# A pairwise-interaction tower on one core: more halves folded, most of them by accumulating transfers, and the sums in another order

## The reference, cut to what matters

```
e = stack([tbl_f[ids[:, f]] for f in range(40)], axis=1)     # 512 x 40 x 64
i_idx, j_idx = triu_indices(40, k=1)                         # 780 pairs
viW = einsum('bpd,pde->bpe', e[:, i_idx, :], W)              # a 64x64 matrix for each pair
z   = einsum('bpe,bpe->bp', viW, e[:, j_idx, :])             # 512 x 780
h = relu(concat([z, dense_ctx]) @ W_top1 + b_top1)           # 796 -> 512
h = relu(h @ W_top2 + b_top2)                                # 512 -> 256
y = h @ W_top3                                               # 256 -> 1
```

## Time and profile before

| | |
|---|---|
| time, median of 3 runs | 334.14 us (334.05 to 335.86) |
| the profiled execution's own time | 336.78 us |
| its span, first to last instruction | 334.9 us |
| granted TensorE clock | 1.00 throughout |
| PE, DVE, ACT, POOL busy | 325.1, 262.9, 199.5, 227.9 us |
| DMA share, mean of 16 engines; moved | 28.77 MB, 86 GB/s |

### The profile page before, as it was taken

The page is one execution under the profiler, slowest core; times in us unless marked ns, Lnnn a source line. Parts: engine busy times, 40 slices in busy tenths (PEclk is TensorE's granted clock), DMA queues, the critical chain, the costliest instruction groups (busy, mean ns, idle before and its releaser), DMA issues.

```text
span 334.9 us, 5224 instructions
## 1 busy us (share of the span) xinstructions
PE 325.1 (97%) x1614; PEld 113.1 (34%) x1614; DVE 262.9 (79%) x245; ACT 199.5 (60%) x1140; POOL 227.9 (68%) x180
## 2 busy tenths in 40 slices
PE   7999999999999999979999999999999999999996
PEld 2244333333333333323333223232333333333342
DVE  2979997786898979848996997968988879888031
ACT  1378633313406794649998993568968495495131
POOL 5665654665667774768888889876996998667000
PEclk9999999999999999999999999999999999999999
DMA  7656331321574754544730320203204000000000
GB/s 190 258 192 217 86 85 20 113 85 25 143 172 88 176 138 89 131 94 135 275 111 18 110 75 6 78 5 116 70 1 113 16 1 0 2 1 0 2 0 0
DMA packets 12479, 28.77 MB, mean 86 GB/s; under 512 B 3730, under 2 KB 4500, under 8 KB 12324
## 3 DMA queue, kind: packets, MB, share of 16 engines
q1 hardware_dynamic: 7060, 20.04, 18.1%
q0 software_dynamic: 5248, 8.40, 12.9%
q10 hardware_dynamic: 144, 0.00, 0.0%
HBM read 24.24 MB, written 0.00 MB: 72 GB/s over the span
## 4 chain that ended last, share of the span: by engine, by line
PE 52%; POOL 18%; DMA 17%; issue 9%; ACT 3%; DVE 1%; POOLq 0%
PE u L665 24%; POOL gath L467 18%; DMA gath<-in_tbl,ids_sb 14%; PE zp L690 8%; PE u L653 6%; PE u L726 4%; PE xp L704 4%; ACT prod L545 2%; PE u L766 2%; DMA prod<-prod 2%; PE u L642 1%; PE xp L610 1%; DMA ids_sb<-in_ids 1%; DVE prod L833 0%; DVE prod L822 0%
## 5 line engine op out<-in xcount | busy, mean ns | idle before, releaser
L833 DVE TENSOR_TENSOR prod<-u,xq_part 128x1024 f32<-128x1024 f32 x148 | 172.6, 1217 | 29.8 <-PE u L665 20.6
L467 POOL DMA_INDIRECT gath<-in_tbl,ids_sb x128 | 126.0, 985 | 69.7 <-DMA gath<-in_tbl,ids_sb 36.5
L665 PE MATMUL u<-xt,w_ring 64*128 64x512 f32 x632 | 162.0, 618 | 0.8 <-DVE prod L833 0.3
L545 ACT ACTIVATE prod<-prod 128x64 f32<-128x64 f32 x512 | 122.7, 242 | 17.0 <-DVE prod L815 12.8
L484 POOL TENSOR_TENSOR prod<-prod 128x1024 f32<-128x1024 f32 x40 | 93.6, 2364 | 10.6 <-DVE prod L833 10.3
L545 ACT ACTIVATION_READ_ACCUMULATOR prod<-prod 128x1 f32 x512 | 96.0, 188 | 0.3 <-issue 0.2
L665 PEld LDWEIGHTS u<-xt,w_ring 64*128 64x128 f32 x632 | 53.3, 185 | 96.4 <-DVE prod L833 40.7
L690 PE MATMUL zp<-prod,sel_sb 128*32 128x512 f32 x480 | 58.5, 599 | 2.5 <-DMA prod<-prod 2.3
L529 ACT ACTIVATE xq_part<-xt 32x512 f32<-32x512 f32 x72 | 45.2, 627 | 1.7
L523 ACT ACTIVATE xt<-xp 128x512 f32<-128x512 f32 x20 | 11.8, 591 | 56.0 <-PE xp L610 44.7
L815 DVE TENSOR_TENSOR prod<-u,gath 128x1024 f32<-128x1024 f32 x32 | 38.9, 1217 | 5.3 <-PE u L653 5.3
(11 more groups left out here) (42 smaller groups left out, 109.0 us busy)
## 6 DMA issues: line engine op xcount, KB each, us to landing
w_ring<-in_w_cell SPq DMA_DIRECT2D x20, 512.0 KB
prod<-prod POOLq DMA_DIRECT2D x8, 512.0 KB
late<-in_ids_small SPq DMA_DIRECT2D x4, 512.0 KB, 5.5
gath<-in_tbl,ids_sb POOLq DMA_INDIRECT x128
wide_w<-in_w_wide SPq DMA_DIRECT2D x8, 256.0 KB
late<-in_w_top SPq DMA_DIRECT2D x1, 1792.0 KB
late<-in_small SPq DMA_DIRECT2D x3, 512.0 KB
wd_sb<-in_w_diag SPq DMA_DIRECT2D x1, 640.0 KB
```

Of the source, the lines that this page charges most:

```text
L467: pool.indirect_dma_start(gath[:, place, t, half, :], None, tables[f], bass.IndirectOffsetOnAxis(ap=ids_sb[:, t, f:f + 1], axis=0),).then_ ...
L545: total = act.activation(part, part, ACT.Copy, accum_out=zw_sb[:, t, 2 * HF * j + pair:2 * HF * j + pair + 1])
L665: mm = pe.matmul(u[:, n % UR, a, :], w_ring[rows, q % RW, at * P:(at + 1) * P], xt[rows, moving % XR, :], start=True, stop=True)
L833: dve.tensor_tensor(prod[:, n % PR, :, :], u[:, n % UR, :, :], x, ALU.mult).then_inc(prod_ready, 1)
```

## The change

Three things change, all by tables and by the order of a list. First, `FOLDED` and `DMA_BELOW`: all units of blocks 12 to 15 are folded, 54 units in all instead of 48. Those of blocks 8 to 15 are folded by transfer, 28 instead of 8; GpSimd's own adds go from 40 to 26. Second, `BATCHES` is sorted by the slot in which a batch can be summed. A plain batch or a quad no longer stands behind a folded one that gets ready later. `places` then puts the rows elsewhere in the banks, and the top weights' rows follow. Third, `FOLDS_AFTER` and `EARLY_AT` are new.

```diff
-FOLDED = {4: 2, 5: 2, 6: 3, 7: 4, 8: 6, 9: 7}
-DMA_BELOW = 6
-FOLDS_AFTER = [0] * 12 + [1, 1, 1, 1, 1, 1, 0, 2, 0, 2, 2, 2, 1, 3, 3, 4, 0, 7, 0, 0]
+FOLDED = {4: 2, 5: 2, 6: 4, 7: 6, 8: 6, 9: 7}
+DMA_BELOW = 8
+FOLDS_AFTER = [0] * 12 + [1, 1, 1, 1, 1, 1, 1, 1, 2, 2, 3, 1, 2, 2, 4, 4, 2, 4, 5, 0]
+LAG = 4
+FOLD_LAG = 12
+def natural_slot(batch):
+    what, m, units, folded = batch
+    last = QUAD_END[m] if what == "quad" else max(AT[("unit",) + u + (HI,)] for u in units)
+    return last + (FOLD_LAG if folded else LAG)
 def batches_in_order():
-    return out
+    return sorted(out, key=natural_slot)
-EARLY_AT = [131, 131, 135, 142, 148, 153, 164, 164, 169, 182, 187, 187]
+EARLY_AT = [129, 140, 140, 144, 147, 147, 166, 166, 166, 181, 184, 193]
```

More of the change, by code:

```diff
@@ L189 @@
 GROUPS = groups()
-LAG = 4
-FOLD_LAG = 12
 def sum_slots():
```

## The result

The changed kernel takes 339.55 us (median of 6, 339.03 to 340.6), the kernel before 335.8 us on the same chip: a ratio of 1.012 [1.0096, 1.0143]. It is slower, by 1.2%. The forecast was 337.0 us, a range of 329 to 343.5, and slower as the likeliest outcome. It was the time before as known then, 334.14 us, plus 2.9; on 335.8 the same 2.9 would have made it 338.7.

A forecast was written before the change was run, and what follows sets the result against it. VectorE was taken to set the pace, with the transfers due before slot 137's round deciding. A delay of +0.25 us there and +2.6 for early steps made +2.9 on 334.14: 337.0 us, range 329 to 343.5.

The forecast's parts named there:

- The mechanism: Up to slot 137: the 10.8 us gained by rounds and order are eaten by waits for transfers on the DMA engines.
- The price of a fold by transfer: DMA engines: one fold by transfer costs 2.75 us, between bounds of 2.6 and 2.9; 20 new ones cost 55 us.
- The first waits: Behind slots 88 and 94: folds beside the top layer's weights last until 168.3 us, and the lead of 6.1 is gone.
- Rounds and order: Slots 39 to 137: fewer rounds and sorted sums gain 6.1 us by slot 82, 10.8 by slot 137, if nothing else waits.
- the ledger: TensorE's lead over VectorE: extra work adds debt, each slot repays 0.27 us, and what exceeds 1.1 us is lost.
- The delay at slot 138: Round behind slot 137 can't start before 223.7 us, when its last transfer is seen; TensorE goes on 0.25 us later.
- rival 3: DMA engines pause between bursts, as a half's gathers must land before the next half's issue: 8.5 us more, 345; 15%.
- The early steps: Behind slot 137: 11 early steps instead of 9, closer together, lose 10.5 us where 7.9 were lost, so 2.6 more.
- rival 2: Transfers bind, but late steps cost nothing, their lost lead covered by earlier waits for ScalarE: 334.4 us; chance 15%.
- The sum: Whole kernel: +0.25 us at slot 138 and +2.6 for the early steps make +2.9, so 337.0 us.
- GpSimd at nothing: GpSimd: 14 adds fewer (33 us less) and 20 issues more (20 us more) costed at nothing; 13 gained if on the path.
- 1: Transfers are never waited for, so 8.2 us are gained: 326 us; 20% for this side as a whole.

## Why the prediction held, and where it didn't

*The mechanism, right.* The order's gain is eaten by waits for the new transfers beside the top layer's weights. The transfers with half their bytes (333.87 us) show that it is the bytes, and the sorted kernel without the 20 new ones (333.63 us, old tables) agrees.

*The price of a fold by transfer, right.* GpSimd's queue had 12.9% of the 16 engines in a span of 334.9 us before, and has 28.5% of 338.3 now. That is 43.2 and 96.4 us, and 53.2 more for 20 transfers: 2.66 us each, against 2.75. (The gathers are on the same queue and are taken to cost the same in both.)

*The first waits, right in place.* Behind slot 94 the folds were to land at 168.3 us, and TensorE started at 169.09. "The lead of 6.1 is gone there" holds and says too little: a lead of 4.6 became 7.1 us behind at slot 95.

*Rounds and order, about right.* Up to slot 82 a gain of 6.1 us was predicted, 4.6 measured; the ledger's 5.7 us of gaps were 6.8. For slots 83 to 137 the ledger has a gain of 4.7. From slot 95 to 107 the changed kernel took 15.06 us where it was 16.73, a gain of 1.7 (the ledger has 1.6 for slots 83 to 107), and from 107 to 138 39.50 where it was 41.86, a gain of 2.4 (3.1 in the ledger), with the waits of 0.90 and 0.26 in it. Half of these 4.0 us are the early steps that moved behind slot 137: with the old places 2.0 are regained (from 173.43 at slot 95 to 230.02 at slot 138, 56.6 us against 58.6). Sorting alone gained hardly anything there (2.2 us at slot 82, 2.6 at slot 138).

*The delay at slot 138, mis-sized: +0.25 predicted, +3.1 measured.* The step was "Even with no pause the last transfer is through at 223.3", a lower bound that I took for the value. The last transfer landed at 226.4 (the chain of the kernel after has it from 213.28 us on, for 13.10 us). The first new one was issued 1.2 us later than I had it (146.19, not 145.0), but the price of 2.66 in place of 2.75 takes 1.8 off. What is left is pauses. The DMA window of the kernel after (length, granted clock, DMA share, GB/s):

```profile
146.50:226.00 79.50, 0.94 0.96 219
```

Four hundredths of 79.5 us are 3.2 us. The longest pause lies in 180 to 185 us, with a share of 0.44: one transfer was issued at 175.12, and the next stood behind the four gathers of the half that followed, until 183.13, and waited for no product. That is the mechanism of rival 3, at less than half its size.

*The path to that delay, and a term left out.* I had TensorE reach slot 137 with its gain and wait there for the last transfer. It waited 0.26 us there. The gain was lost at slots 88 and 94, 11.7 us between slots 82 and 95, and 2.2 to 2.3 of these are the clock, which was not in my sum at all. I had worked out the landing at 168.3 and didn't carry it on. Shown is that the stall suffices by itself: 7.54 us of waiting and the clock at half behind it lead to the same place (228.54) in a kernel with 16 transfers, the last of them issued at 175.16 us. The two bounds, the stall carried on and the last transfer, fall almost on one point: behind slots 133 and 137 only 1.2 us of waits are left.

*The early steps, mis-sized: +2.6 predicted, +0.3 measured.* From slot 139 to the end of the slots VectorE's gaps add up to 11.5 us where the ledger has 10.5; the longest is that behind slot 166 (3.59, and 3.4 in the ledger). So for the new places the ledger was about right. But before, the gaps there add up to 10.8, not 7.9. The largest that the ledger lacks is one of 1.60 us at slot 140; what it waited for, the trace doesn't tell plainly. Right behind it TensorE waited for ScalarE's copy. TensorE's timeline of the kernel before:

```profile
230.43 1.13 PE L704 MATMUL xp<-late 128*128 128x512 f32 x2 [0.63 <-ACT xt L523]
```

The changed kernel has neither. With the old early steps it has the wait for ScalarE again (0.70 us), with a gap of VectorE of 1.36 behind it. So what the new places lose was lost before too, in part to ScalarE, which is what rival 2 said: it was nearly right in this half.

*The sum, right by two errors.* +0.25 and +2.6 are 2.9; +3.1 and +0.3 are 3.4, the growth of the span in the two traces; the medians give 3.75. That it came so near is luck in the parts.

*GpSimd at nothing, right here.* Its adds wait more for products (13.7 us, 10.3 before), and it is less busy (213.7 us, 227.9 before). With 38 adds in place of 26 it is late once, by 2.42 us, and the time is 1.004.

*Rivals.* 1 is refuted: rounds wait 10.4 us for transfers. 2 failed on the transfers' part (+3.1 by slot 138, not the 0.25 that it shares with my sum). 3, pauses of the DMA engines, holds for 3.2 us of the 8.5 that it had, and for more with the weights earlier.

What stays open: how much of the stall at slot 94 is the plain queueing of bytes, and how much the way in which the two queues share the engines. A kernel whose weights come in small pieces between the folds would tell; it wasn't tried. Open is also why two of the three places of the weights cost 3 to 4 us more than the third, with a longest wait of like length.

## What to carry to other kernels

Work that is moved to the DMA engines isn't free because they were at 0.29: add up what must land before each point that waits for it, and look above all at the one large load that falls in between, since a chain of dependent transfers beside it stalled at each of the three places tried (6.78, 7.08 and 8.67 us). In the kernel with 16 transfers and the weights late, where the load came behind the last of them, no such stall stood. A change to the order of work and one that loads a shared resource should be timed apart; here one gains 0.6% and the other takes it back three times over. Where the clock falls in a wait, its price is more than the wait; at slot 94 it was 2.3 us more.

## What the runs showed of the hardware

*The clock fell after short waits too, and not always.* Rounds took 1.93 or 1.94 us, not 1.06, after 7.08, 4.95, 4.14, 3.01, 2.72, 2.42 and 2.05 us without a matmul, but 1.06 or 1.07 after 2.04, 2.17, 2.56, 2.68 and 3.27. After the 2.56 (top layer's weights later) and the 3.27 (weights earlier) the clock did fall, only behind the round: it was 0.63 from 228.5 to 233 us, where three slots took 4.34 us from start to start in place of 2.68, and 0.60 from 198.7 to 200 us. So a fall can come after the first work behind a wait. After 2.04 and 2.17 it didn't come at all, nor after 2.68, where idle matmuls stood in the wait ahead of it. The 2.04, 2.05 and 2.17 are all the wait behind slot 88, at 155.2 to 155.5 us. So the length of the idle time alone didn't decide.

*A transfer that adds, on-chip to on-chip, 128 rows of 4 KB, takes 2.66 us of all 16 engines (packet time),* 1.6 times a load of as many bytes from memory (1.7 us from the earlier trace rows). Issue to landing is 4.7 us for the quickest, 7.4 in the median and 15.1 for the longest, that of slot 94, which shared the engines with 2.3 MB of weights on another queue. The Trainium skill ("DMA: Bandwidth & Descriptors", Queues, rings and completion order) says that each engine takes turns between the queues that have work for it, packet by packet; a fold that is drawn out to three times its own time beside another queue's load agrees with that.
